# A ring of seven one-bank buffers, spans of 512 queries and a product on GpSimd, in a four-layer attention and mixture-of-experts kernel

## What is computed

```python
x = x + attn_a(norm(x))    # 16 heads of 8; softmax over ALL keys, then the causal mask, then times V
x = x + ffn(norm(x))       # router over 8 experts, top 2, plus a shared expert, all SwiGLU 128-128-128
x = x + attn_b(norm(x))    # 16 heads of 8, rotary embedding, softmax, output projection and bias
x = x + ffn(norm(x))
# ffn: p = softmax(x @ router_w); sel = top_k(p + expert_bias, 2); y_e = (silu(x @ w1[e]) * (x @ w3[e])) @ w2[e]
#      out = shared(x) + sum over selected e of p[e] * y_e
```

## Time and profile before

| | |
|---|---|
| median of 3 runs | 2003.87 us (1995.84 to 2017.19) |
| profiled execution | 2010.94 us |
| its span | 2009.2 us |
| mean granted clock of TensorE | 0.944 |
| busy PE, DVE, ACT, POOL | 1857.0, 1571.9, 1447.1, 715.7 us |
| first exponent, last exponent | 136.36 us, 1918.55 us |

### The profile page before, as it was taken

How to read it: one execution, slowest core, us unless ns; L and a number is a source line. 1 busy time by engine, 2 the same in 40 slices (tenths; PEclk the granted TensorE clock), 3 DMA queues, 4 the chain that set the end, 5 groups by cost and what they waited for, 6 DMA issues and landing times.

```text
span 2009.2 us, 42496 instructions
## 1 busy us (share of the span) xinstructions
PE 1857.0 (92%) x16784; PEld 884.3 (44%) x16784; DVE 1571.9 (78%) x2030; ACT 1447.1 (72%) x2890; POOL 715.7 (36%) x984
## 2 busy tenths in 40 slices
PE   2889999999999999999989999999998999999988
PEld 1344443444444444444444444444444444444467
DVE  3779999988969789888888888888878888887132
ACT  1238888877667776777877787776786778778765
POOL 4222223344634446444452322323222222322244
PEclk7559999999969999999999999989999999999999
DMA  5220100000100001001010010101000000000000
GB/s 178 110 111 18 46 19 18 19 17 18 49 18 16 35 18 49 18 18 41 11 48 17 17 49 18 38 13 48 17 23 18 23 13 20 10 2 8 1 6 17
DMA packets 38087, 61.79 MB, mean 31 GB/s; under 512 B 4352, under 2 KB 19328, under 8 KB 37760
## 3 DMA queue, kind: packets, MB, share of 16 engines
q1 hardware_dynamic: 37888, 59.07, 8.3%
HBM read 30.74 MB, written 27.26 MB: 29 GB/s over the span
## 4 chain that ended last, share of the span: by engine, by line
PE 69%; DVE 18%; ACT 6%; issue 5%; POOL 1%; DMA 1%; SPq 0%; POOLq 0%; DVEq 0%; ACTq 0%
PE ps_sum L1181 22%; PE ps_two L1124 16%; DVE negmax L915 11%; PE ps_one L1148 5%; PE ps_one L1219 5%; PE ps_two L1201 4%; PE ps_one L1201 4%; PE ps_sum L1219 3%; DVE silu L961 2%; PE ps_sum L1201 2%; PE ps_sum L1148 2%; ACT probs L760 1%; DVE xn L935 1%; PE ps_two L1095 1%; PE ps_one L1103 1%
## 5 line engine op out<-in xcount | busy, mean ns | idle before, releaser
L915 DVE TENSOR_REDUCE negmax<-ps_two 128x2 f32<-128x1024 f32 x1024 | 1223.0, 1220 | 227.8 <-PE ps_two L1124 222.7
L760 ACT ACTIVATE probs<-ps_one 128x512 f32<-128x512 f32 x1382 | 783.0, 603 | 150.6 <-PE ps_one L1148 90.4
L1124 PE MATMUL ps_two<-kx,qx 24*128 24x512 f32 x2048 | 528.9, 518 | 71.1 <-DVE negmax L915 50.9
L1148 PE MATMUL ps_one<-qx,kx 26*128 26x512 f32 x1382 | 567.6, 505 | 6.8 <-ACT first L801 4.1
L1181 PE MATMUL ps_sum<-probs,vg 128*9 128x256 f32 (+1 forms) x6144 | 474.4, 382 | 7.1 <-ACT sums L767 5.6
L760 ACT ACTIVATE probs<-ps_sum 128x512 f32<-128x512 f32 x666 | 401.6, 603 | 91.9 <-PE ps_one L1148 68.4
L1124 PEld LDWEIGHTS ps_two<-kx,qx 24*128 24x128 f32 x2048 | 194.8, 189 | 444.3 <-DVE negmax L915 194.8
L648 POOL TENSOR_SCALAR scaled<-scaled,gates 128x128 f32<-128x128 f32 x468 | 173.6, 390 | 516.8 <-ACT scaled L825 516.6
L1148 PE MATMUL ps_sum<-qx,kx 26*128 26x512 f32 x666 | 336.1, 505 | 4.4 <-ACT first L801 3.2
L1148 PEld LDWEIGHTS ps_one<-qx,kx 26*128 26x128 f32 x1382 | 216.5, 184 | 61.9 <-ACT probs L760 33.3
L627 POOL TENSOR_TENSOR pdiag<-probs,causal 128x512 f32<-128x512 f32 x128 | 166.4, 1301 | 181.5 <-ACT probs L760 181.4
(11 more groups left out here) (153 smaller groups left out, 1883.4 us busy)
## 6 DMA issues: line engine op xcount, KB each, us to landing
qk_rows<-limbs SPq DMA_DIRECT2D x36, 512.0 KB, 3.3
qx<-qk_rows SPq DMA_DIRECT2D x128, 96.0 KB
kx<-qk_rows SPq DMA_DIRECT2D x128, 96.0 KB
qk_rows<-prod_c SPq DMA_DIRECT2D x8, 512.0 KB, 3.7
qx<-mlimbs SPq DMA_DIRECT2D x256, 4.0 KB
qk_rows<-prod_s SPq DMA_DIRECT2D x4, 512.0 KB, 2.9
out_dram<-x SPq DMA_DIRECT2D x8, 256.0 KB, 2.3
x<-in_x SPq DMA_DIRECT2D x3, 512.0 KB, 6.1
```

The source lines that it names most:

```text
L760: act.activation(m.probs[:, blk % PROB_SLOTS, EXP_HEADS[k], :], bank, ACT.Exp, scale=SCALE).then_inc(s.freed[ONE], 1)
L915: dve.tensor_reduce(m.negmax[:, unit // UNITS % 2, half, first:first + NT + 1:NT], ps.rearrange("p (h k) -> p h k", h=2), AX.X, ALU.max, n ...
L1124: last = pe.matmul(slot[:, bank * CHUNK:(bank + 1) * CHUNK], m.qx[rows, n % SLOTS, i * P:(i + 1) * P], m.kx[rows, n % SLOTS, half * CHUNK: ...
L1148: pe.matmul(bank, m.kx[rows, n % SLOTS, j * P:(j + 1) * P], m.qx[rows, n % SLOTS, half * CHUNK:(half + 1) * CHUNK], start=True, stop=True) ...
```

## The change

- **Spans of 512 queries.** A span p is one group and one half of its queries, in the order batch, half, group: 64 spans of 16 units, each with a combining, a transposing and a loading of maxima of its own. `LEAD` goes from 46 to 30. A group's two spans are four apart, so `load(n + 4)` is issued behind the last exponent of group n's second span: 18 steps ahead of the scores of the group that takes its slot.
- **One ring of seven banks** in place of the two. Every item takes one bank, the next, and waits for the reader, whichever engine, of the item seven before. Scores are two items of one bank each, with a reduction of 128x512 each; the rotary products are four items.
- **The product with `first` moves to GpSimd.** VectorE forms (tanh + 1) times h3 from PSUM in one instruction, GpSimd multiplies it by `first`, which now has two buffers, one step later (`hidden`); h3 comes three steps behind h1, and y seven.
- **Projections.** Chunks 0 to 3 are projected in front of the first scores, chunks 4 to 7 at steps 6, 22, 38 and 54.
- **Feed-forward.** The chunks of the last layer from the fifth on are routed one by one, the pace is 5 steps behind step 800, and 15 units are left for the end. There VectorE multiplies the second product by the gate and adds it to x out of PSUM (`mix`); ScalarE and GpSimd have no part in that.
- The order of a step (side work, two scores, two exponents, weighing) stays. The copy of q and k out of DRAM is written with its axes in another order.

The diff, cut to its core:

```diff
-UNITS = NT * HALVES * 2
-BLOCKS = HALVES * NT
-EXPS = BLOCKS * GH
-TOTAL = 2 * GROUPS * UNITS
+SPANS = GROUPS * HALVES
+UNITS = CT * HALVES * 2
+TOTAL = 2 * SPANS * UNITS
...
-E_BANKS = 3
+BANKS = 7
 WEIGH_LAG = 2
 FILL_AT = 3
-LEAD = 46
+LEAD = 30
 TURN_AT = 2
-PACE = 7
 X_SLOTS = 3
+PACE, LATE_PACE, LATE_FROM = 7, 5, 800
...
+def place(p):
+
+    layer, of_layer = divmod(p, SPANS)
+    b, of_batch = divmod(of_layer, NG * HALVES)
+    half, g = divmod(of_batch, NG)
+    return layer * GROUPS + b * NG + g, half
...
+    return staged(at, (0, ("h1", k)), (3, ("h3", k)), (4, ("hidden", k)), (7, ("y", k)), (9, ("gate", k)))
...
+    side = {110: [("bweights",)]}
+    for c in range(CT, CHUNKS):
+        add_side(side, projected_a(c, 6 + 16 * (c - CT)))
+    ready, of_chunk = [], NG * UNITS
+    for b in range(B):
+        more, at = routed(1, b * HALVES, HALVES, (b + 1) * HALVES * of_chunk + 11)
+        add_side(side, more)
+        ready += [at] * HALVES
+    for c in range(CHUNKS - 1):
+        at = (CHUNKS + c + 1) * of_chunk + 9
+        add_side(side, mixed_heads(c, at))
+        width = HALVES if c < CHUNKS // 2 else 1
+        if (c + 1) % width == 0:
+            more, at = routed(3, c + 1 - width, width, at + 8 - 3 * (width - 1))
+            add_side(side, more)
+            ready += [at] * width
+    free = 0
+    for chunk, at in enumerate(ready):
+        for e in range(NE):
+            free = max(free, at)
+            if free + 9 >= TOTAL:
+                break
+            add_side(side, feed_forward(chunk * NE + e, free))
+            free += PACE if free < LATE_FROM else LATE_PACE
+        if chunk < CHUNKS:
+            add_side(side, projected_b(chunk, free + 14))
+    for p in range(2 * SPANS - 1):
+        add_side(side, {(p + 1) * UNITS + 2 * WEIGH_LAG + 3: [("sums", p)]})
...
+    items = [("scores", unit, i) for i in range(2)]
...
-        if step % UNITS == 0 and n and n + SLOTS - 1 < 2 * GROUPS:
-            items.append(("load", n + SLOTS - 1))
+        if step % UNITS == 0 and step:
+            n, half = place(step // UNITS - 1)
+            if half == HALVES - 1 and n + SLOTS < 2 * GROUPS:
+                items.append(("load", n + SLOTS))
...
+    plan = []
+    for first in range(0, CT, 2):
+        pair = range(first, first + 2)
+        plan += [(kind, 0, c) for c in pair for kind in ("stats", "moments")]
+        plan += [("apply", 0, c) for c in pair]
+        plan += [(kind, 0, c) for c in pair for kind in ("turn", "q", "k", "low", "store")]
+        plan += [("v", 0, c) for c in pair]
+        plan += [("load", 0)] if not first else [("wsplit",), ("load", 1)]
+    side = {6: [("load", 2)], 16: [("load", 3)], UNITS + TURN_AT + 1: [("maxima", 0)]}
...
+    stages = [[("oturn", c)], [("omix", c), ("oadd", c)], [("stats", 3, c), ("moments", 3, c), ("apply", 3, c)],
+              [("turn", 3, c)], [("logits", 3, c)], [("chain", 3, c, 1, k) for k in range(CHAIN)]]
+    side = {}
+    for i, stage in enumerate(stages):
+        add_side(side, {1 + i * (late - 1) // len(stages): stage})
     items += [("h1", done), ("h3", done)]
     for i, k in enumerate(units):
         items += side.get(i, [])
         if i + 1 < len(units):
             items += [("h1", k + 1), ("h3", k + 1)]
-        items += [("y", k), ("gate", k)]
+        items.append(("mix", k))
...
+    def held_by(self, *item):
+
+        i = self.ring[item] - BANKS
+        return self.order[i] if i >= 0 else None
...
+    ps_banks = ctx.enter_context(nc.psum_tensor("ps_banks", [P, BANKS, CHUNK], F32))
+    ps_sum = ctx.enter_context(nc.psum_tensor("ps_sum", [P, CHUNK], F32))
+    m.banks = tuple(ps_banks[:, i, :] for i in range(BANKS))
+    m.acc = ps_sum[:, :]
...
+    def first_into_hidden(k):
+
+        pool.wait_ge(s.freed[VECTOR], counts.use("h3", k) + 1)
+        pool.wait_ge(s.freed[SCALAR], counts.use("h1", k) + 1)
+        pool.tensor_tensor(m.hid[:, k % 2, :], m.hid[:, k % 2, :], m.first[:, k % 2, :], ALU.mult
+                           ).then_inc(s.hidden, 1)
...
+    def take_max(unit, k):
+        bank = take(("scores", unit, k))
+        i, half = divmod(unit % UNITS // 2, HALVES)
+        col = heads_of(unit)[k] * CT + i
+        dve.tensor_reduce(m.negmax[:, unit // UNITS % 2, half, col:col + 1], bank, AX.X, ALU.max, negate=True
+                          ).then_inc(s.freed[VECTOR], 1)
...
-            dve.tensor_tensor(m.hid[:, k % 2, :], m.silu[:, k % 2, :], ps[:, 0:CHUNK], ALU.mult
-                              ).then_inc(s.freed[TWO], 1)
+            tail = ("mix", k - 2) in counts.kind["mix"]
+            done = ("mix", k - 2) if tail else ("y", k - 2)
+            dve.wait_ge(s.filled[READER[done[0]]], counts.use(*done) + 1)
+        dve.wait_ge(s.freed[SCALAR], counts.use("h1", k) + 1)
+        if ("hidden", k) in counts.kind["hidden"]:
+            dve.scalar_tensor_tensor(m.hid[:, k % 2, :], m.silu[:, k % 2, :], 1.0, bank, ALU.add, ALU.mult
...
+    def add_mixed(k):
+
+        bank = take(("mix", k))
+        layer, c, e = ffn_unit(k)
+        dve.wait_ge(s.gated, counts.chains[(layer, c)] + 1)
+        dve.wait_ge(s.constants, 1)
+        dve.wait_ge(s.added, counts.added_before(("mix", k), plan))
+        i = counts.nth("mix", k)
+        if i:
+            dve.wait_ge(s.mixed, i)
+        for t in range(CT):
+            tile = c * CT + t
+            x = m.x[:, tile_cols(tile)]
+            last = dve.scalar_tensor_tensor(x, bank[:, t * D:(t + 1) * D], m.gates[:, tile, e:e + 1], x,
+                                            ALU.mult, ALU.add)
+        last.then_inc(s.mixed, 1)
+        dve.wait_ge(s.mixed, i + 1)
+        dve.sem_inc(s.freed[VECTOR], 1)
...
-        count = counts.use(*item)
-        if count >= E_BANKS:
-            pe.wait_ge(s.freed[ONE], count - E_BANKS + 1)
-        return m.one[count % E_BANKS]
-
-    def slot_of(item):
-
-        count = counts.use(*item)
-        if count >= 2:
-            pe.wait_ge(s.freed[TWO], count - 1)
-        return m.two[count % 2]
+        holder = counts.held_by(*item)
+        if holder:
+            pe.wait_ge(s.freed[READER[holder[0]]], counts.use(*holder) + 1)
+        return m.banks[counts.bank(*item)]
 
     def turn(layer, c):
...
+        h = heads_of(unit)[k]
+        rows = slice(TILE_ROWS * h, TILE_ROWS * h + ROWS)
+        pe.matmul(bank_of(("scores", unit, k)), m.qx[rows, n % SLOTS, tile * P:(tile + 1) * P],
+                  m.kx[rows, n % SLOTS, half * CHUNK:(half + 1) * CHUNK], start=True, stop=True
+                  ).then_inc(s.filled[VECTOR], 1)
```

More of the change, by code:

```diff
@@ L60 @@
 STORES = 3
-ONE, TWO = "one bank", "two banks"
-RING = {"turn": ONE, "q": ONE, "k": ONE, "v": ONE, "logits": ONE, "h1": ONE, "y": ONE, "exp": ONE, "oturn": ONE, "omix": ONE,
-        "maxima": ONE, "sums": ONE,
-        "qk": TWO, "scores": TWO, "h3": TWO}
+SCALAR, VECTOR = "read by ScalarE", "read by VectorE"
+READER = {"turn": SCALAR, "q": SCALAR, "k": SCALAR, "v": SCALAR, "logits": SCALAR, "h1": SCALAR, "y": SCALAR,
+          "exp": SCALAR, "oturn": SCALAR, "omix": SCALAR, "maxima": SCALAR, "sums": SCALAR,
+          "qk": VECTOR, "scores": VECTOR, "h3": VECTOR, "mix": VECTOR}
 class Buffers:
@@ L237, in begun @@
     for unit in range(LEAD):
         plan += side.get(unit, []) + scores_of(unit)
-    for unit in range(LEAD, max(side) + 1):
-        plan += side.get(unit, [])
     return plan
 def ended(done):
-    last, n = 2 * GROUPS * BLOCKS, 2 * GROUPS - 1
+    last, p, c = 2 * SPANS * NT, 2 * SPANS - 1, CHUNKS - 1
     items = [("weigh", blk, part) for blk in range(last - WEIGH_LAG, last) for part in range(2)]
-    items += [("copy", n, HALVES - 1), ("sums", n, HALVES - 1)]
-    side, units = {}, list(range(done, 2 * LAYER_UNITS))
@@ L251, in ended @@
-    for h in range(HALVES):
-        c = CHUNKS - HALVES + h
-        add_side(side, {1 + h: [("oturn", c)], 2 + h: [("omix", c), ("oadd", c)]})
-        add_side(side, {4 + h: [("stats", 3, c), ("moments", 3, c)], 5 + h: [("apply", 3, c)],
-                        6 + h: [("turn", 3, c)], 7 + h: [("logits", 3, c)]})
-    add_side(side, {9: [("chain", 3, B - 1, k) for k in range(CHAIN)]})
-    late = 2 * LAYER_UNITS - FFN_UNITS - done
-    assert late > 2
-    side = {at * late // 10: [item for k in side if k * late // 10 == at * late // 10 for item in side[k]]
-            for at in sorted(side)}
+    items += [("copy", p), ("sums", p)]
@@ L309, in use, with bank, added_before @@
     def use(self, *item):
-        return self.uses[RING[item[0]]][item]
+        return self.uses[READER[item[0]]][item]
+    def bank(self, *item):
+        return self.ring[item] % BANKS
+    def held_by(self, *item):
+        i = self.ring[item] - BANKS
+        return self.order[i] if i >= 0 else None
+    def added_before(self, item, plan):
+        return sum(1 for other in plan[:plan.index(item)] if other[0] in ("gate", "oadd"))
     def nth(self, *item):
@@ L656, in add_scaled @@
         x = m.x[:, chunk_cols(c)]
[L657 removed]
```

(23 more changed lines are left out.)

477 lines of the change are left out of this document (211 added, 266 removed).

## The result

The changed kernel takes 2014.99 us (median of 20 runs; the kernel before 2006.97, also 20): the ratio is 1.0052, with a 95% interval of 1.0031 to 1.0073. It is half a percent slower, where 4% faster was forecast. Some executions of a kernel are slower than its others, at a lower granted clock; the times and ratios of this document are of the others, and only the kept trace of number 12 is of such an execution.

What follows compares the result with a forecast made beforehand. TensorE was taken to bound the middle, held up by small rings on both sides. Terms -58 + 15 + 10 - 36 + 35 + 20 - 70 = -84 took the median from 2003.87 to 1920 us, range 1850 to 2010.

Steps and rivals of the forecast that it cites:

- Prologue, -58: Stretch before the first exponent: to end at 78 us in place of 136.4, -58 us (-48 to -62).
- Tail, -36: Feed-forward units after the last exponent: 15 left instead of 27, 54 us in place of 90, -36 us.
- The ring, -70: Middle: with an item waiting for the one seven before, half of TensorE's waits for ScalarE go, -70 us (0 to -150).
- the second exponent's wait, +20: Middle: second exponent waits for the bank of the previous step's first score; +20 us with VectorE's pace (-30 to +90).
- My sign that the clock would fall oftener: Whole run: prediction is wrong if the clock falls oftener for stretches like that at 557 us; no size given.
- projections +15: Middle: four projections moved into steps cost TensorE +15 us (0 to 25).
- maxima +10: Middle: twice as many maxima, with 32 more transposes, cost TensorE +10 us (0 to +15).
- units moved +35: Middle: 12 feed-forward units moved in from the end cost +35 us (0 if they filled idle time).
- reductions and product +20: Middle: shorter reductions (+70 us of VectorE) and the product leaving VectorE (-99); +20 us on TensorE, second exponent's wait included.
- The price of a short reduction: VectorE: a 512-element reduction takes about 0.68 us, spaced at 0.60; a unit costs +0.07 us, +70 us in the middle.
- The rival "VectorE holds the exponents": Middle: second exponent waits for VectorE's first reduction of the step before; 2060 us, middle from 1877 us on; 13%.
- "GpSimd's product comes late": Feed-forward units: TensorE's second product waits behind GpSimd's mask and gate, +77 us, 1997 us; 8%.

Runs made afterwards that it cites:

- number 12: Number 3 with the second score of a step moved behind the weighing; 2222.6 us, ratio 1.1070 to the kernel before.
- number 1: Changed kernel with its seven banks divided into two rings, three for ScalarE and four for VectorE; 1933.4 us, ratio 0.9633 to the kernel before.
- number 3: Changed kernel, one ring of seven, with each step's two exponents issued in front of its two scores; 1912.2 us, ratio 0.9511 to the kernel before.
- number 5: Kernel before with each 128x1024 reduction split into two of 128x512; 2034.9 us, ratio 1.0136 to the kernel before.
- number 8: Number 3 with the product with first moved back from GpSimd to VectorE; 1958.6 us, ratio 0.9767 to the kernel before.
- number 11: Changed kernel, scores in front, with the product with first moved back to VectorE; 2114.5 us, ratio 1.0549 to the kernel before.
- number 9: Changed kernel with a ring of six banks instead of seven; 2272.0 us, ratio 1.1342 to the kernel before.

## Why the prediction was wrong

- **Prologue, -58:** right in kind, measured -66. The first exponent is at 70.2 us; I had 78, with 74 as the least. The first scores came 3 us earlier than 38.9 and the maxima's road did not hold up the rest.
- **Tail, -36:** measured -33. Fifteen units in 57.5 us, where I had 54.
- **The ring, -70, together with the second exponent's wait, +20, is the step that failed.** I credited every item with "1.75 steps back", an average of the clean step, though by the same places the second exponent is one step back, behind VectorE's first reduction. I saw that wait, and sized it at +20 with the reductions and the product. It is nearly all of the new wait: second exponents account for 176 of the 191 us, 138 of them in clean steps. I left out that in a step with a side item the first exponent too is one step back; that is a real gap, but a small one (14 us). Measured from number 1 (two rings, all else changed) the merging cost +79 us in the middle as it was ordered, and -25 in number 3. The mechanism that I forecast, exponents freed from ScalarE, does occur: those waits went from 137 to under 20 us. A larger wait took their place.
- **The clock.** My sign that the clock would fall oftener came true, 26 stretches in the middle for 15 and 163 us for 103, though none as long as the one at 557 us. The sum had no term for it; about a quarter of the middle's +101 comes with it.
- **The rest of the middle** (projections +15, maxima +10, units moved +35, reductions and product +20: +80) was too dear. Number 1, whose rings are of the sizes of before, has the middle at 1805 us, +22. Which of the four was too high was not taken apart, except that the split of reductions by itself is +22 in the middle (number 5), and the product's move is worth 46 us in number 3's order (number 8). The expectation of number 8 speaks of my letting 30 of 99 us reach the end; the prediction states no such share.
- **The price of a short reduction** was right: 0.681 us alone and (2.47 - 0.68)/3 = 0.60 us from one to the next, as read from L970 and the row behind it. The estimate of 0.658 us from the cycles that the Trainium skill gives (VectorE: DVE Perf Modes, section The TRN2 errata) is near the duration, 3% under. By durations a unit would cost +0.125 us; in number 5 VectorE's busy time rises by 58 us for 1024 units, 0.06 each, as the spacing has it. My remark that this figure would put the time 55 us above mine let all of VectorE's 54 us more reach the end, which my own sum did not do for its 70.
- **The rival "VectorE holds the exponents"**, at 13%, names what happened, with its place (the second exponent of a step) and its turning point: a middle of 1877 us; it is 1884. Its price of 2060 us was 45 too high, as it had the exponents' relief at nothing and the small work too dear. I gave it too little by weighing VectorE's load, and not how far its first reduction of the step before lies behind when the second exponent is due.
- **"GpSimd's product comes late":** no. Second products idle for 0.8 us in all behind it. Nor do scores wait for a load anywhere behind the prologue.

## What to carry to other kernels

When rings of buffers are merged, write out for every item which item it waits for, in the clean step and in each step that has a side item, and see which *reader* gives that buffer back and when, item by item and not on average; a reader that runs near its limit should not be one step back from what stands in the in-order queue. The order of issue within a step is then a free choice worth percents in a shared ring (4.9% faster or half a percent slower here), and worth nothing or a loss with rings of their own. Products that run beside each other must also stay neighbours in the queue.

## What the runs showed of the hardware

- The same 115 us of VectorE's time (129 x 0.889) cost 46 us in one order of issue and 99.5 us in the other.
- The granted clock differs between kernels of the same work: 0.975 over the span of number 3 (1906 us), 0.948 in the changed kernel (2012 us), 0.935 in number 11 (2099 us), 0.89 in number 9 (2272 us). In these it is lower the more exponents wait, and part of what a wait costs comes as stretches at 1.2 GHz. It does not go with waits alone: number 12, whose TensorE is busy for 98% of the kept trace, has 0.88 and 0.89 in the two executions behind its ratio. Which is cause and which is effect these runs don't tell apart.
- A small VectorE instruction with two SBUF operands waits for GpSimd. The combining of 16 columns (L947) takes 0.17 to 0.18 us in 36 places of the changed kernel. In the other 28 it takes 0.22 to 1.21 us, and in every one of these it ends 0.02 to 0.04 us behind the end of an instruction that GpSimd is at. The 0.94 us at 1703.93 is such a case: GpSimd is at the very product that was moved to it, from 1703.56 for 1.28 us, to 1704.84, and VectorE's instruction ends at 1704.87. It holds up the reduction that the exponent at 1705.52 waits for. With 64 of them the mean is 0.434 us; before, with 32 columns, it was 0.289 us. So GpSimd's product takes back a little of what it gives.
